# First layer of a two-layer graph network: group sums issued ahead of the third edge layer, and added on VectorE ahead of the products

## The reference, cut to what matters

```python
h = gelu(edge_scalar_attr @ Wfc1 / sqrt(8))        # 8 -> 64
h = gelu(h @ Wfc2 / sqrt(64))                      # 64 -> 64
w = h @ Wfc3 / sqrt(64)                            # 64 -> 192, in four parts w0..w3
gs, gv = f_s[edge_src], f_v[edge_src]              # gathered rows of the source nodes
mid0 = w0 * gs * y0 ;  mid1 = w3 * (gv . y1) ;  mid2 = w1 * gs * y1 ;  mid3 = w2 * gv * y0
agg  = segment_sum(mid, edge_dst)                  # sums over the edges of a node
x    = layernorm(x + skip(x) + alpha * (agg @ Wl2))
```

## Time and profile before

| what | us |
|---|---|
| median of 3 runs | 2632.79 |
| lowest and highest run | 2631.97, 2643.34 |
| span of the profiled execution, first to last instruction (the page gives no other time for it) | 3060.6 |
| first gather of the first layer starts (profiled) | 51.60 |
| last gather of the first layer starts (profiled) | 1462.00 |
| last `products` of the first layer start (profiled) | 1478.21 |
| first scatter of the second layer starts (profiled) | 1523.64 |

### The profile page before, as it was taken

How to read it: one execution, slowest core, us unless ns; L and a number is a source line. 1 busy time by engine, 2 the same in 40 slices (tenths; PEclk the granted TensorE clock), 3 DMA queues, 4 the chain that set the end, 5 groups by cost and what they waited for, 6 DMA issues and landing times.

```text
span 3060.6 us, 78767 instructions
## 1 busy us (share of the span) xinstructions
PE 2639.6 (86%) x24556; PEld 1983.6 (65%) x24556; DVE 1645.1 (54%) x4537; ACT 984.7 (32%) x2591; POOL 2008.3 (66%) x1630
## 2 busy tenths in 40 slices
PE   7667777886768877876799999999999999999997
PEld 4334444443434444443588888888888888888883
DVE  3446434443444444444466666666666666666664
ACT  2212212221221221221244444444444444444442
POOL 4555554555555555555188888888888888888885
PEclk5566656657676566566699999999999999999998
DMA  6233332332233233332388888888888888888877
GB/s 193 59 96 93 86 89 77 89 93 79 82 93 83 81 95 82 86 94 80 83 140 141 141 141 140 141 141 139 141 141 140 140 140 142 140 140 140 141 136 176
DMA packets 392755, 356.11 MB, mean 116 GB/s; under 512 B 60112, under 2 KB 343440, under 8 KB 392368
## 3 DMA queue, kind: packets, MB, share of 16 engines
q0 software_dynamic: 150528, 141.40, 32.0%
q1 hardware_dynamic: 237552, 208.10, 24.3%
q10 hardware_dynamic: 4544, 4.93, 0.5%
HBM read 246.44 MB, written 133.44 MB: 124 GB/s over the span
## 4 chain that ended last, share of the span: by engine, by line
PE 77%; issue 9%; another core or an unknown queue 8%; DVE 2%; ACT 2%; DMA 1%; POOL 1%; SPq 0%; ACTq 0%; DVEq 0%; POOLq 0%
PE ps_o L1051 11%; PE ps_w L1039 10%; PE ps_d L1060 8%; PE ps_o L1049 8%; PE ps_w L901 7%; PE ps_pg L842 6%; PE ps_x L1073 6%; PE ps_h L894 6%; PE ps_h L888 3%; PE ps_x L1013 3%; PE ps_pg L857 2%; PE ps_pg L851 1%; PE ps_pg L854 1%; PE ps_nd L917 1%
## 5 line engine op out<-in xcount | busy, mean ns | idle before, releaser
L623 POOL DMA_INDIRECT tab<-summed,sidx x784 | 1223.2, 1560 | 284.4 <-issue 230.8
L605 POOL DMA_INDIRECT gat<-f,gidx x784 | 753.4, 961 | 694.7 <-DVE feats L1358 384.9
L1498 DVE TENSOR_TENSOR prod<-ps_w,xg 128x768 f32<-128x768 f32 x392 | 375.4, 958 | 266.3 <-PE ps_w L1039 252.7
L1051 PE MATMUL ps_o<-ro_v,prod 128*128 128x96 f32 x3136 | 479.1, 275 | 0.0
L842 PE MATMUL ps_pg<-feats,sel 128*32 128x320 f32 x1568 | 225.9, 661 | 265.7 <-issue 265.5
L1051 PEld LDWEIGHTS ps_o<-ro_v,prod 128*128 128x128 f32 x3136 | 414.1, 192 | 0.0
L797 ACT ACTIVATE xg<-ps_x 128x768 f32<-128x768 f32 x392 | 296.4, 808 | 341.3 <-PE ps_x L1073 340.3
L1039 PE MATMUL ps_w<-hid,wf 64*128 64x128 f32 x4704 | 368.7, 289 | 2.0 <-ACT hid L798 2.0
L1049 PE MATMUL ps_o<-ro_s,prod 96*128 96x96 f32 x1568 | 327.5, 291 | 19.0 <-DVE msg L1509 4.8
L1039 PEld LDWEIGHTS ps_w<-hid,wf 64*128 64x128 f32 x4704 | 293.5, 187 | 70.2 <-issue 44.6
L1060 PE MATMUL ps_d<-msg,same 128*128 128x193 f32 x1568 | 332.3, 334 | 0.7 <-ACT summed L816 0.7
(11 more groups left out here) (262 smaller groups left out, 3451.0 us busy)
## 6 DMA issues: line engine op xcount, KB each, us to landing
xt<-in_src_rows SPq DMA_DIRECT2D x196, 256.0 KB
xt<-feat SPq DMA_DIRECT2D x784, 36.0 KB
xt<-in_ea SPq DMA_DIRECT2D x196, 128.0 KB
feat<-xt SPq DMA_DIRECT2D x25, 576.0 KB
hot_dst<-in_dst_rows SPq DMA_DIRECT2D x98, 128.0 KB
gat<-f,gidx POOLq DMA_INDIRECT x784
hot_dir<-sh_rows SPq DMA_DIRECT2D x98, 128.0 KB
xt<-hot_dst SPq DMA_DIRECT2D x196, 64.0 KB
```

The source lines that it names most:

```text
L605: pool.indirect_dma_start(out=gat[:, r % 4, k, :], out_offset=None, in_=t["f0"], in_offset=bass.IndirectOffsetOnAxis(ap=gidx[:, r // 4, at ...
L623: pool.indirect_dma_start(out=t["tabs"][into[k]], out_offset=bass.IndirectOffsetOnAxis(ap=sidx[:, r, k:k + 1], axis=0), in_=summed[:, r, k ...
L1051: last = pe.matmul(ps_o[:, k, 96 + 64 * c:192 + 64 * c], prod[:, ur % 2, k, 1 + c, :], ro_v[:, c, :], start=True, stop=True)
L1498: dve.tensor_tensor(prod[:, r % 2, :, :, :].rearrange("p k c e -> p k (c e)"), ps_w4[:, :, 0:3 * P], xg[:, r // 2, r % 2 * 2:r % 2 * 2 + 2 ...
```

## The change

On TensorE `window_sums(s-3)` with its three waits is issued before `layer3(s-1)` and not after it. On DVE `add_window(s-2)`, with its register load and its two waits, is issued before `products(s)` and not after it; `positions(s)` stays behind both. No instruction is added or removed, and the banks, the buffers and the waits' counts are the same.

```diff
@@ TensorE, step(s)
                         if runs(s, NGRP):
                             layer2(s, r)
-                        v, _, vr = lagged(s, j, r, 1, 2)
-                        if runs(v, NGRP):
-                            layer3(v, vr)
                         if runs(u, NGRP):
                             pe.wait_ge(part_done, u + 1)
                             pe.wait_ge(place_ready, u + 1)
                             since(pe, acc_done, u)
                             window_sums(pe, parts[:, ur, :], place[:, ur, :, :], ur, agg_done)
+                        v, _, vr = lagged(s, j, r, 1, 2)
+                        if runs(v, NGRP):
+                            layer3(v, vr)
@@ DVE, step(s)
                         if runs(s, NGRP):
                             since(dve, part_ready, s - 1)
                             select(s, r % 2, pad_off[:, bass.ds(s * G, G)], s + 1)
-                            products(s, j, r)
                         u, _, ur = lagged(s, j, r, 2, 4)
                         if runs(u, NGRP):
                             base = dve.value_load(base_i[0:1, bass.ds(u, 1)], min_val=0, max_val=N)
                             dve.wait_ge(agg_done, u + 1)
                             since(dve, acc_done, u)
                             add_window(ur % 2, base)
                         if runs(s, NGRP):
+                            products(s, j, r)
                             positions(r % 2, slot_rel[:, bass.ds(s, 1)])
```

## The result

The median rose from 2632.38 us (4 runs, 2628.57 to 2643.34) to 2681.03 us (4 runs, 2680.86 to 2717.62): a ratio of 1.0199, with a 95% interval of 1.0152 to 1.0245. The change makes the kernel slower by 48.7 us, where the prediction had 2628 us and a range from 2615 to 2643. The profiled execution of after took 2680.86 us, with a span of 2678.8.

The account below looks back on a forecast made before the run. It took POOL's gathers as the bound of the first layer in the timed runs. From 2632.8 us it took off 2.5 for the layer's end and 2.0 for the backlog: 2628 us, range 2615 to 2643.

Parts of the forecast that it names:

- what bounds the kernel: First layer, timed runs: POOL's gathers set the pace, 5.02 us a group; back to back they give 2617.9 to 2624.5 us.
- the loop: layer3, products, addition, tile_sums: cutting it was priced at 73 to 194 us, paid only where it sets the pace.
- the fall of 70 or more: Sign in the profile after: the 265.7 us idle before tile_sums (L842) become less by some 70 or more.
- The first rival: The loop sets the pace in timed runs too; cutting it gains 138 us, giving 2495, up to 2618; chance 0.25.
- the layer's end: End of the first layer: the last tile_sums starts at about 1480.5 and not 1483.05, 2.5 us saved.
- the backlog: Up to three groups still ahead of the consumers at the last gather, each shorter: 1.1 to 3.0 us, taken as 2.0.
- profiled span: Sign in the profile after: the span falls to around 2990 us even if the median does not.
- POOL's waits: Sign in the profile after: POOL's waits for products, 422.7 us in the first layer before, fall with the profiled span.
- `window_sums` ahead of `layer3`: On TensorE: layer2 covers the wait for the copy of the sums, so cost nothing; without cover 0.44 us a group.
- 1.78 us to spare: TensorE's spare time per group: 5.02 us of gathers against 3.24 of work at 2.4 GHz, before and after.
- The slower rival: Spare time in one piece puts more groups at 1.2 GHz, 0.61 us each; half the groups give 2693 us; chance 0.10.
- The third rival: TensorE's clock stays at 2.4 GHz in the first layer, 3.8 us a group, giving 2386 us; chance 0.03.

Follow-up runs that it names:

- second profile: The unchanged kernel profiled again with no edit, for a trace without long stops: 2646.52 us, span 2644.5 us.
- half-gathers kernels: Two of four gathers per group left out, of the unchanged kernel (2599.29 us) and of the one with only VectorE's part of the change (2566.01 us).
- e3_dve_part: VectorE's part of the change alone (add_window ahead of products) on the unchanged kernel, TensorE as before: 2639.41 us, ratio 0.9998.
- first profile: The profile of the unchanged kernel read for the prediction, with long stops; its span was 427.8 us longer than the median.
- e2: TensorE's part of the change alone (window_sums ahead of layer3) on the unchanged kernel, VectorE as before: 2989.8 us, ratio 1.1333.
- e7: VectorE's part alone plus eight filler matmuls between layer2 and layer3, layer3's waits ahead of layer2: 2791.88 us.
- e8: VectorE's part alone plus the same eight filler matmuls ahead of layer2, layer3's waits also ahead of layer2: 2657.33 us, ratio 1.002.
- e10: The changed kernel with eight filler matmuls added behind layer3, window_sums still between layers 2 and 3: 2775.2 us, ratio 1.0527.
- e1: The unchanged kernel run and profiled again with no edit: 2646.52 us (1 run).
- e4: The unchanged kernel with layer3 issued ahead of layer2 on TensorE, nothing else changed: 2627.9 us, ratio 0.9965.
- e11: The unchanged kernel with two of the four gathers of each group left out: 2599.29 us, ratio 0.986.
- e12: VectorE's part of the change alone, with two of the four gathers of each group left out: 2566.01 us, ratio 0.973.
- e5: The changed kernel with window_sums moved further ahead, before layer2, so layers 2 and 3 are adjacent but window_sums wait for the copy: 2976.85 us.
- e9: The kernel with window_sums ahead of layer2 (e5) plus eight filler matmuls behind layer3: 2785.8 us, ratio 1.0567.
- e6: The changed kernel with one more 128x128 matmul ahead of layer3, its output overwritten by layer3: 2998.1 us, ratio 1.1347.

## Why the prediction was wrong, step by step

**Right, but by a small margin: what bounds the kernel.** The gathers do, in the runs that are timed. Shown by POOL's 29.0 us of waits in the second profile, and by the half-gathers kernels, which also show how near the next bound is: without half of the gathers only 41 us are gained.

**Right: VectorE's part.** It cuts the loop (idle ahead of `tile_sums`, by the page's line, 125.0 us in e3_dve_part and 162.4 in the unchanged kernel, half of the fall of 70 or more that was foretold), and it gains nothing, as gathers set the pace: 0.9998 alone. The first rival, in which the loop sets the pace of the timed runs and 138 us are gained, is out; the loop's gain is 33 us even with half of the gathers gone. The 4.5 us for the layer's end and the backlog are below what the time of e3_dve_part can tell: its interval goes from -6.3 to +5.5 us (0.9976 and 1.0021 of 2639). The traces show the end of the layer, though. The last `tile_sums`, first of the unchanged kernel, then of after:

```profile
1079.64 1.30 PE L842 MATMUL ps_pg<-feats,sel 128*32 128x320 f32 x8 [0.57 <-issue]
1116.72 0.74 PE L842 MATMUL ps_pg<-feats,sel 128*32 128x320 f32 x8 [0.57 <-issue]
```

They start 4.92 and 2.76 us after the last products (1074.72 and 1113.96), so 2.2 us are saved of the 2.5 in the sum.

**Signs that told nothing.** The profiled span of after, 2678.8 us, is far from the 2990 foretold, because this execution has none of the long stops. For the same reason POOL's waits fell against the first profile (422.7 to 67.4 us), while against the second they rose (29.0 to 67.4).

**The step that failed:** "`window_sums` ahead of `layer3`. [...] I cost it at nothing". The dependency was read rightly: `layer2` covers the copy, and there is no wait in the chain of after. But the price was not a wait. Put between layers 2 and 3, the window sums lower the granted clock of TensorE in the first layer from 0.83 to 0.67. The same work takes 140.8 us more, and the spare time covers 102.3 of them. It measured 38 us in POOL's waits and 39 in the layer's length; 48.7 in the medians.

**Why it was not covered.** The prediction gave TensorE "1.78 us to spare", at 2.4 GHz. That holds only where that clock is granted; at 1.2 GHz its own 5.67 us of work leave nothing of 5.02. Over the layer, with its mixture of both levels, the half-gathers kernels show 4.96 us a group, and 4.80 with the loop cut, against 5.02 for the gathers: 0.06 to 0.22 to spare. At 1.2 GHz after takes 5.60, so in a long stretch at that level the gathers fall behind by 0.58 us with every group.

**The slower rival** had the cause right, more groups at 1.2 GHz, and a price near the measured one (0.61 us a group, against 0.58). That the two prices agree is in part luck: its 0.61 is counted from a mean group of 5.06 us, and not from the gathers. Its reason was not borne out: it asked for spare time in one piece, and from 674.2 to 776.6 us after stayed at 0.50 with no spare time at all. Over the layer TensorE is idle for 1046.92 - 967.68 = 79 us, where the unchanged kernel is idle for 182. "TensorE's work and its spare time are the same before and after" was the argument against it, and it doesn't reach the order of the work.

**The third rival** rested on a rule of the Trainium skill (TensorE: Matmul & The Clock Gate, A second HAM failure mode: psum-queue depth-cycling), that small idle times make the clock swing. Read as the prediction reads it, fewer such idle times should give more clock. Here idle time fell by more than half, in part because the same work took longer, and the clock was lower; from 690 to 770 us it stayed at 0.50 with no idle time at all. The measurement decides: in this layer the order of the matmuls counts for more than the gaps between them.

**What is shown and what is open.** Shown: it is TensorE's part alone that costs (e2, e3); it works through the clock (rows of after, e2, e7); and the place of small matmuls in the step changes the granted clock with the same work and the same waits (e7 against e8). The record of the clock agrees across the profiled executions. Where small matmuls stand between layers 2 and 3, a stretch at 0.50 lasts 39 to 89 us on average (after, e2, e7, e10). Where the two layers are side by side and no wait for the copy stands in the group, it lasts 10 to 12 us (e1, e3, e4, e8, e11, e12). Argued only: the summary that the clock comes up where layers 2 and 3 stand side by side, with neither a wait nor `layer1` close by. It fits e4, e5, e8, e9 (29 us) and e10; it was formed after e5 had felled a simpler form of it, and e6 is not explained by it. Which property of those matmuls the chip answers to is open.

## What to carry to other kernels

Reordering matmuls on a TensorE that swings between its two clock levels need not be free even where every dependency is covered: before and after, compare the granted clock of the stretch and the mean duration of one unchanged matmul, not the idle time. Spare time must be counted at the clock that is granted over the stage, not at the faster level. If a profiled span is far from the timed median, profile again before building on its stops.

## What the runs showed of the hardware that was not expected

- A TensorE busy for 80.00 of 80.00 us stayed at 0.50 all the while (after, 690 to 770 us); over a whole layer of 1343.65 us it was 0.50 with 90% busy (e5_sums_first).
- A stretch at 0.50 lasted 45.9 us on average in one order of the same matmuls and 11.8 in the other (after, e1_before).
- The same 10884 matmuls were run at 0.69 or at 0.83, by the place of eight small ones in each group (e7, e8).
- Added work made a kernel faster: eight small matmuls more in each group, and 71 us less or more than that (2800.61, the slower of e9, against 2872.01, the fastest of e5).
- The two parts of one change can be worth 0 and -350 us alone and -49 together (e3, e2, after).
